# A products buffer laid out with the eight products of an output element side by side

## The reference

```python
def xattn(k, v, q, ssm_kernel, D, head_dim=8):     # k = v = context, q = layernorm(x)
    kv = jnp.einsum('bhil,bhjl->bijhl', k_, v_)    # 8 x 8 products per head and position
    y  = irfft(rfft(kv, 1024) * rfft(ssm_kernel, 1024))[..., :512]   # causal convolution along l
    out = y + kv * D
    return jnp.einsum('bijhl,bhil->bjhl', out, q_)  # sum over i
x = x + xattn(...)
x = x + moe_ffn(layernorm(x))     # shared expert + top 4 of 16 experts, capacity 256
```

## Time and profile before

| | us |
|---|---|
| median of 3 runs | 693.5 (691.5 to 695.0) |
| the profiled execution | 693.3 |
| its span in the profile | 691.5 |
| TensorE busy | 616.1 (89%) |
| VectorE busy | 567.5 (82%) |
| GpSimd busy | 434.7 (63%) |
| ScalarE busy | 282.0 (41%) |
| reductions of line 1206, 32 of them | 123.8 |
| products of lines 1187 and 1190, 540 of them | 145.1 |

### The profile page before, as it was taken

One profiled execution on the slowest core, in us unless ns is written; L12 is line 12 of the kernel. 1 busy time (PEld: TensorE's weight loads), 2 busy tenths in 40 slices (PEclk: granted clock), 3 DMA queues, 4 the chain that ended last, 5 costly groups with the idle time before them and its releaser, 6 DMA issues.

```text
span 691.5 us, 14342 instructions
## 1 busy us (share of the span) xinstructions
PE 616.1 (89%) x4487; PEld 571.8 (83%) x4487; DVE 567.5 (82%) x1248; ACT 282.0 (41%) x503; POOL 434.7 (63%) x499
## 2 busy tenths in 40 slices
PE   2856998999999999999998888998999999999990
PEld 2846896998989989999898676988988888888880
DVE  5899989769889889788899687988888888888740
ACT  3422542423433424234241144355465565544640
POOL 4875697566766667576721116477667777777662
PEclk9987999999999999999999899999999999999996
DMA  6572512404225224131210326766767777776434
GB/s 168 175 212 85 183 32 78 136 33 129 86 61 152 61 78 134 61 91 56 71 57 1 91 96 205 252 180 194 208 193 200 202 216 227 218 207 186 104 39 54
DMA packets 50373, 90.12 MB, mean 130 GB/s; under 512 B 3921, under 2 KB 20305, under 8 KB 50337
## 3 DMA queue, kind: packets, MB, share of 16 engines
q1 hardware_dynamic: 43168, 72.89, 34.0%
q0 software_dynamic: 7168, 16.78, 11.6%
HBM read 72.71 MB, written 16.94 MB: 130 GB/s over the span
## 4 chain that ended last, share of the span: by engine, by line
PE 51%; issue 20%; DVE 15%; ACT 6%; POOL 4%; DVEq 2%; DMA 1%; SPq 0%; ACTq 0%; POOLq 0%
PE gu L527 15%; PE yb L464 14%; PE gu L552 8%; PE gu L656 5%; PE mb L444 3%; ACT ew L865 3%; PE mb L671 2%; DVE ew L1473 2%; DVE prod L1187 2%; PE yb L656 2%; DVE mid L1489 1%; DVE xgT L1481 1%; DVE prod L1190 1%; DVE oT L1206 1%; POOL midl L1009 1%
## 5 line engine op out<-in xcount | busy, mean ns | idle before, releaser
L464 PE MATMUL yb<-kvh,toep 128*128 128x288 f32 x640 | 141.4, 308 | 10.5 <-DVE prod L1190 10.5
L527 PE MATMUL gu<-xT,sw 128*128 128x256 f32 (+2 forms) x1152 | 143.2, 283 | 3.7 <-issue 3.1
L527 PEld LDWEIGHTS gu<-xT,sw 128*128 128x128 f32 (+2 forms) x1152 | 138.8, 182 | 4.5 <-issue 4.1
L1206 DVE TENSOR_REDUCE oT<-prod 128x256 f32<-128x2048 f32 x32 | 123.8, 3870 | 0.1
L464 PEld LDWEIGHTS yb<-kvh,toep 128*128 128x128 f32 x640 | 110.6, 199 | 12.3 <-issue 10.7
L1001 POOL TENSOR_TENSOR kvl<-kv,kvh 128x1152 fp32r<-128x1152 f32 x31 | 83.4, 2689 | 52.0 <-ACT kvh L753 51.9
L1473 DVE TENSOR_TENSOR ew<-raw_w,ew 128x704 fp32r<-128x704 f32 x64 | 108.5, 1700 | 4.6 <-ACT ew L865 4.6
L993 POOL TENSOR_TENSOR kv<-kT 128x256 f32 (+3 forms) x248 | 111.2, 490 | 0.0
L464 PE MATMUL yb<-kvl,toep 128*128 128x288 f32 x320 | 97.9, 306 | 0.0
L1187 DVE TENSOR_TENSOR prod<-yb,qT 128x96 f32<-128x96 f32 (+11 forms) x288 | 78.1, 282 | 22.8 <-PE yb L464 21.2
L1009 POOL TENSOR_TENSOR midl<-mid,midh 128x256 fp32r<-128x256 f32 x40 | 33.3, 835 | 74.6 <-ACT midh L769 64.5
(11 more groups left out here) (170 smaller groups left out, 1084.8 us busy)
## 6 DMA issues: line engine op xcount, KB each, us to landing
toep<-toeplitz_taps SPq DMA_DIRECT2D x32, 512.0 KB, 3.7
raw_w<-in_L_ffn_w_gate_dram SPq DMA_DIRECT2D x16, 704.0 KB
raw_w<-in_L_ffn_w_up_dram SPq DMA_DIRECT2D x16, 704.0 KB
raw_d<-in_L_ffn_w_down_dram SPq DMA_DIRECT2D x16, 512.0 KB
c_t<-in_ctx_dram SPq DMA_DIRECT2D x16, 256.0 KB, 4.6
x_t<-in_x_dram SPq DMA_DIRECT2D x16, 256.0 KB, 5.1
normalised_tokens<-xn SPq DMA_DIRECT2D x16, 256.0 KB, 3.0
out_dram<-yo SPq DMA_DIRECT2D x16, 256.0 KB, 2.9
```

Source lines behind the costliest of these rows:

```text
L464: last = pe.matmul(yb[:, lb, 0:PW], toep[s][:, a, d:d + P], rhs[:, s, m, :], start=(i == 0), stop=(i == len(steps) - 1))
L527: last = pe.matmul(gu[0:m, i % 2, u * GT:(u + 1) * GT], sw[:, c, a, col:col + m], xT[:, c, b, :], start=(c == 0 and (a, b) == PASSES[0]), ...
L1206: dve.tensor_reduce(oT[:, :, hl * HD * B:(hl + 1) * HD * B], prod[:, s, :, :, :].rearrange("p c i w -> p c w i"), AX.X, ALU.add)\
```

## The change

The last two dimensions of `prod` change places: [128, 2, 4, 64, 8], the eight products of an output element side by side. The sum reads the buffer in order, without a rearranged view. Each product is written with a step of 8 floats (32 bytes). The count of instructions, their operands otherwise, every wait and every order stay as they are.

```diff
-        prod = place("prod", [P, 2, LB, HD, HD * B], fp32)
+        prod = place("prod", [P, 2, LB, HD * B, HD], fp32)
...
-                        last = dve.tensor_tensor(prod[:, s, lo:hi, d, d * B:HD * B],
+                        last = dve.tensor_tensor(prod[:, s, lo:hi, d * B:HD * B, d],
                                                  yb[:, lo:hi, POFF[d]:POFF[d] + w], q[:, lo:hi, 0:w], ALU.mult)
                         if d:
-                            last = dve.tensor_tensor(prod[:, s, lo:hi, HD - d, 0:w],
+                            last = dve.tensor_tensor(prod[:, s, lo:hi, 0:w, HD - d],
                                                      yb[:, lo:hi, POFF[d]:POFF[d] + w], q[:, lo:hi, d * B:HD * B],
                                                      ALU.mult)
...
                 dve.tensor_reduce(oT[:, :, hl * HD * B:(hl + 1) * HD * B],
-                                  prod[:, s, :, :, :].rearrange("p c i w -> p c w i"), AX.X, ALU.add)\
+                                  prod[:, s, :, :, :], AX.X, ALU.add)\
                     .then_inc(d_sum, 1)
```

## The result

The changed kernel takes **682.5 us** (median of 4 runs, 681.2 to 682.7) against 693.6 us on the same chip. The ratio is 0.985, 95% interval 0.982 to 0.987. It is faster by 11 us, clear of the noise. In the experiments one slow execution, of `pad_first` (714.6 us at a mean granted clock of 0.926, its others 0.966 to 0.976), is left out of its median. The forecast was 692.7 us, no difference; the range ended at 683.0, half a microsecond above. The result is where rival 1 stood (683.7 us), though not for its reason: the stepped write is not cheap.

What follows compares the result with a forecast made beforehand. VectorE was taken to bound the first heads, a second stretch to about 92 us and the last head, TensorE the regular groups. Three terms of -0.2 us summed to -0.6 us from 693.3: 692.7 us, range 683 to 708.

Steps and rivals of the forecast that it cites:

- rival 1: Stepped product writes cost nothing or little, so the three places on the path save 9.6 us: 683.7 us; chance 0.19.
- The sum: VectorE reduction over 2048 elements, once per head: reading in order takes it from 3.87 to 2.27 us, saving 1.60 us.
- last head: End of the stage: products later by 1.37 us, sum shorter by 1.60 us, so -0.2 us.
- the regular groups: 119.7 to 345.8 us, five periods of 45.2 us: TensorE covers VectorE's work, so nothing is gained or lost.
- 2.3 us of room: Head 3's products end 2.3 us before TensorE wants their PSUM banks, enough for the 1.37 us added.
- the variance that GpSimd waits for: End of the first VectorE stretch: GpSimd takes it over at 67.51 us, claimed to stay within 1 us of there.
- Part 2: Added cost of the products: 2048 stepped writes per head at 0.67 ns extra each, 1.37 us per head.
- first stretch: 22.46 to 67.4 us, VectorE without a gap: 4.5 heads of products at +1.37, four sums at -1.60, together -0.2 us.
- second stretch: 67.4 to 92 us: the chain returns to VectorE for head 5's sum and head 6's products, -0.2 us.
- rival 2: Stepped writes dearer than at 64 bytes, and products hold the PSUM banks: slower, about 704 us; chance 0.25.
- the estimate of +18 us: Total if the skill page's 2.50 ns for a 24-word output step held, products gaining 2.9 us a head.
- passes through: 92 to 119.7 us, work of ScalarE, GpSimd and TensorE: the earlier shift was to carry on through it.

Runs made afterwards that it cites:

- pad_first: Changed kernel plus a 1024-element reduction (1.13 us) ahead of the sum in each of heads 0 to 3 alone: 689.2 us, 0.996 of the kernel before.
- Experiment 2: Changed kernel plus an extra reduction ahead of every sum, rebuilding the VectorE time per head that was predicted: 693.0 us, 1.000 of the kernel before.
- the series: Changed kernel with VectorE multiplications and reductions at many write and read steps ahead of its own work: 693.2 us including them, a single execution.
- padded: Changed kernel plus a reduction ahead of every sum, 1024 elements in heads 0 to 3, 512 in the others: 693.0 us, 1.000 of the kernel before.
- step_only: Changed kernel keeping the stepped product writes, but its sum reads numbers 64 floats apart as before: 702.0 us, 1.015 of the kernel before.
- rows8: Changed kernel with products in runs of eight floats and the sum reading 8 floats apart: 697.9 us, 1.008 of the kernel before.
- experiment 3: Changed kernel plus a 1024-element reduction in heads 0 to 3 alone (689.2 us) or head 7 alone (683.3 us); changed kernel again: 682.0 us.

## Why the prediction was wrong

**What held.** The sum: 2.27 us forecast, 2274 ns measured. Most of the map of stages: VectorE counts in the first groups and at the last head, the regular groups are TensorE's and give nothing (45.2 us before and after), and 2.3 us of room cover the longer pass. Experiment 2 shows that the gain hangs on VectorE's time per head: with that put back, it is gone (693.0 us). It does not test which places count, since a meeting of 2.5 us and a clock worth 1.6 us come into its total. One sign failed: the variance that GpSimd waits for was to be taken over within 1 us of 67.51 us. It is ready at 60.7 and taken over at 62.23.

**The step that failed** is Part 2, "the extra is 0.67 ns, so 2048 x 0.67 = 1.37 us per head". The price of one stepped write was right or even low (0.78 ns in the series). It was added to the time of the instruction, but it runs beside the start of the next. I had the row for it, two instructions on `V` that overlap by 0.31 us, and used it only for the end of the range. Measured: 0.3 us where the instructions have at most 128 elements, 1.0 where they have up to 256. With these, the sum of the prediction would have been:
- first stretch: 3 x 0.25 + 0.73 for the passes, 0.2 for the half of head 0, less 6.4: -4.7 us (forecast -0.2);
- second stretch: 0.9 - 1.6 = -0.7 us; the two together -5.4, measured -5.5;
- last head: 1.0 - 1.6 = -0.6 us, measured -0.7 (8.7 to 9.4 in the table).

That is 6.0 us, 687.3 us, and a forecast of "faster". That the first two agree so well is partly luck: VectorE had gained 6.7 us at the sum of head 4 (60.63 against 67.35) and only 4.8 at that of head 5 (72.42 against 77.25), as it now waits 2.5 us for ScalarE between them. Small slips in the working change nothing of this: the rows give an extra of 0.66 ns, not 0.67; rival 2's terms start at +7 us, not +8; and the estimate of +18 us is +9 with its own three places, the rest being regular heads.

**What was missing: 4.6 us** (the two below make 4.4; 0.2 us stay unassigned)**.** First, a place on the path, 1.6 us: between the rows of 5.5 and 7.1 us of the table lies the sum of head 7. The chain of before shows 2.79 us at 104.10 as "issue". VectorE was in that sum, and the product `mid` behind it releases GpSimd's last remainder and with it `down`. The sum, `mid` and the first `down` in order of time, before and after:

```profile
102.24 3.83 DVE L1206 TENSOR_REDUCE oT<-prod 128x256 f32<-128x2048 f32 x1
...
105.99 0.41 DVE L1235 TENSOR_TENSOR mid<-sil,gu 128x256 f32<-128x256 f32 x1
...
108.44 0.47 PE L543 MATMUL gu<-sd,midh 128*128 128x512 f32 x1 [1.22 <-POOL midl L1009]
```
```profile
96.68 2.28 DVE L1206 TENSOR_REDUCE oT<-prod 128x256 f32<-128x2048 f32 x1
...
98.88 0.41 DVE L1235 TENSOR_TENSOR mid<-sil,gu 128x256 f32<-128x256 f32 x1
...
101.32 0.47 PE L543 MATMUL gu<-sd,midh 128*128 128x512 f32 x1 [0.78 <-POOL midl L1009]
```

The sum starts 5.6 us earlier, `mid` and `down` 7.1. I wrote that the shift "passes through" from 92 us on. A stretch of "issue" in the chain has to be looked up in the order of time.

Second, TensorE's clock, 2.8 us. The same 15 matmuls of `down`, in the chain of waits of the kernel before, at both places, then of the changed one:

```profile
109.34 5.23 PE gu L552 x15
...
379.52 5.07 PE gu L552 x15
```
```profile
102.22 3.62 PE gu L552 x15
...
369.96 3.62 PE gu L552 x15
```

Between 109.3 and 112.0 us the clock granted was 0.54, near the lower level of 1.2 GHz; in the changed kernel it is 1.00 throughout. The two falls cost 1.6 and 1.45 us, of which 1.2 us of the second remain by the experts. What decides this clock stays open. The waits ahead of `down` do not tell it. The kernel before idles for 1.22 us behind 1.09 us of transposes at the first place and falls; `padded`, `step_only` and `rows8` have the same 1.22 and 1.09 us there and keep the full clock (3.64 to 3.65 us). At the second place `pad_first` has the waits of the changed kernel (1.13 us ahead of the transposes, 0.53 behind them) and takes 5.01 us against 3.62.

Nor does the kernel alone decide it. Beside the experiments the kernel before ran 36 times: 14 executions with a mean granted clock of 0.968 or more took 689.6 to 691.2 us, the 22 with a lower one 691.1 to 695.1, medians 690.8 and 693.4. The profiled one (693.3 us, 0.967) belongs to the second kind. The changed kernel's ten executions had 0.969 to 0.980. So the 2.8 us are what this pair of profiles shows, and not a price of the layout that every execution pays.

The subtraction that no longer meets GpSimd's remainder brought 2.0 us to VectorE, but little to the end. VectorE then waited 0.81 us for a convolution, and GpSimd, which the weights' DMA and ScalarE hold up, had its own end at 62.27 us behind VectorE's 60.7. In `pad_first`, where VectorE is late again, little of it arrives at `down` either (experiment 3).

**The range** missed by half a microsecond. It took rival 1 as the sum of three places, with nothing below it for a fourth place or for the clock.

## What to carry to other kernels

Price a stepped operand against an instruction's start, not per element alone: measure from start to start, and many short instructions hide what a few long ones show. Keep the eight values of a sum, and the writes that make them, within steps of 2 floats, or in runs of two, where the layout allows. Before calling a part of the path covered, look up each stretch of "issue" in the order of time. Where one engine is late ahead of TensorE, more than its own time can come back: here the clock came on top, in the profiled executions. And a shift of a microsecond can make the subtractions of two engines meet, which cost 2 to 2.5 us a time here and looks like a price of the change.

## What the runs showed of the hardware

- VectorE, fp32, steps of 4 to 12 floats cost a write 0.7 to 0.8 ns per element, 16 to 64 floats 0.6, but 24 floats 1.5 to 2.0; 2 floats nothing, 3 floats 0.3. Reading in a reduction: 4 and 8 floats 0.60 us for 256 elements, 16 and 64 floats 0.58, 1 and 2 floats 0.42. So a step of 32 bytes is no better than one of 256 (4160 against 3870 ns for 2048 elements).
- Stepped writes of one VectorE instruction run on under the start of the next: fifteen more instructions in a head cost 0.3 us in place of 1.0.
- VectorE's subtraction of two SBUF operands beside GpSimd's remainder: 3.35 us instead of 0.88 for one instruction of 704 elements, in the kernel before. Where it runs beside GpSimd's pair products, those take 4.83 us instead of 3.53.
- TensorE's `down` behind 1.22 us of idle time ran at a granted clock of 0.54 in the kernel before and at the full one in three others with the same wait; it moves a total by some 1.5 us at each place. The mean granted clock differs between executions of one kernel (0.959 to 0.973 in the kernel before).
